# Macaron block on one Trainium2 core: two halves of a split in one slot tile, a last unit in pieces of two batches, and instruction lists anew

## The reference, cut to what matters

```python
x = L0_attn_hidden_states                       # (8, 256, 128)
x = x + 0.5 * ffn(layernorm(x))
x = x + attn(layernorm(x))
x = x + 0.5 * ffn(layernorm(x))                 # same weights again

def ffn(x):                                     # 8 experts, top 2, capacity 40 per batch
    probs = softmax(x @ Wr); topk_probs, topk_experts = top_k(probs, 2)
    pos = position of the token among those of its expert (cumulative count); keep = pos < 40
    buf[e, b, pos] += x                         # dispatch
    h = relu(einsum('ebnc,ech->ebnh', buf, W1) + b1)
    y = einsum('ebnh,ehc->ebnc', h, W2) + b2
    return sum over k of y[e, b, pos] * keep * topk_probs

def attn(x):                                    # 16 heads, feature dim 16, head dim 8
    q, k, v = x @ Wq / 4, x @ Wk, x @ Wv
    # quadratic attention, causal: weights (q.k)**2, normalised by their sum + 1e-5
    return o @ Wo
```

## Time and profile before

| | |
|---|---|
| median of 3 runs | 193.42 us (193.16 to 193.84) |
| profiled execution | 193.27 us, span 191.5 us, granted TensorE clock 1.0 |
| PE busy | 179.5 us (94%), 2253 matmuls |
| ACT busy | 150.4 us (79%) |
| DVE busy | 135.6 us (71%) |
| POOL busy | 66.5 us (35%) |

### The profile page before, as it was taken

One profiled execution on the slowest core, in us unless ns is written; L12 is line 12 of the kernel. 1 busy time (PEld: TensorE's weight loads), 2 busy tenths in 40 slices (PEclk: granted clock), 3 DMA queues, 4 the chain that ended last, 5 costly groups with the idle time before them and its releaser, 6 DMA issues.

```text
span 191.5 us, 5890 instructions
## 1 busy us (share of the span) xinstructions
PE 179.5 (94%) x2253; PEld 139.4 (73%) x2253; DVE 135.6 (71%) x400; ACT 150.4 (79%) x357; POOL 66.5 (35%) x102
## 2 busy tenths in 40 slices
PE   7976999999999999999999899999999999999962
PEld 7954899799979855555555555555599998999952
DVE  0999858968888588559466676879488887365162
ACT  3788999768768698998998889898799675993830
POOL 8904762800000036654854558679300000000000
PEclk9999999999999999999999999999999999999999
DMA  4999900530016896379476825614400008003003
GB/s 139 330 326 316 230 15 0 99 69 3 0 35 187 221 239 204 106 201 240 133 207 194 236 80 157 184 45 82 82 3 0 3 0 168 0 5 109 0 5 110
DMA packets 34284, 22.82 MB, mean 119 GB/s; under 512 B 14248, under 2 KB 31184, under 8 KB 34256
## 3 DMA queue, kind: packets, MB, share of 16 engines
q1 hardware_dynamic: 34112, 22.44, 44.5%
q10 hardware_dynamic: 144, 0.00, 0.0%
HBM read 14.05 MB, written 5.24 MB: 101 GB/s over the span
## 4 chain that ended last, share of the span: by engine, by line
PE 84%; DVE 8%; ACT 4%; issue 1%; POOL 1%; DVEq 0%; ACTq 0%; POOLq 0%
PE psB L1007 18%; PE psB L1077 9%; PE psS L1060 6%; PE psS L888 5%; PE psB L898 5%; PE psS L890 4%; PE psS L889 4%; PE psB L983 4%; PE psB L1079 4%; PE psB L1098 3%; PE psB L1016 3%; PE psB L950 2%; PE psB L888 2%; PE psB L1088 2%; PE psB L890 2%; PE psB L889 2%
## 5 line engine op out<-in xcount | busy, mean ns | idle before, releaser
L554 POOL TENSOR_SCALAR_AFFINE_SELECT amat<-amat 128x512 f32<-128x512 f32 x64 | 44.1, 697 | 55.4 <-ACT amat L637 54.5
L637 ACT ACTIVATE amat<-psS 128x768 f32<-128x768 f32 x64 | 50.1, 820 | 5.8 <-PE psS L1062 5.3
L608 ACT ACTIVATE hid<-psS,biasT 128x160 f32<-128x160 f32 x128 | 39.9, 404 | 9.6 <-PE psB L1007 4.8
L1007 PE MATMUL psB<-hid,w 128*128 128x160 f32 x256 | 40.4, 305 | 0.3 <-issue 0.2
L1007 PEld LDWEIGHTS psB<-hid,w 128*128 128x128 f32 x256 | 35.5, 190 | 1.4 <-issue 1.1
L888 PE MATMUL psS<-xe,w 128*128 128x160 f16 x128 | 27.1, 232 | 1.6 <-DVE xe L343 1.3
L889 PE MATMUL psS<-xe,w 128*128 128x160 f16 x128 | 27.1, 233 | 0.0
L890 PE MATMUL psS<-xe,w 128*128 128x160 f16 x128 | 27.1, 233 | 0.0
L1077 PE MATMUL psB<-amat,vst 128*32 128x256 f32 x256 | 20.4, 390 | 0.0
L1060 PE MATMUL psS<-stack 64*128 64x256 f16 x128 | 17.3, 278 | 0.9 <-ACT amat L637 0.8
L616 ACT ACTIVATE yT<-psB,biasT 128x160 f32<-128x160 f32 x32 | 12.6, 413 | 6.6 <-PE psB L1007 6.5
(11 more groups left out here) (151 smaller groups left out, 349.9 us busy)
## 6 DMA issues: line engine op xcount, KB each, us to landing
qk_parts<-qk SPq DMA_DIRECT2D x16, 256.0 KB, 3.5
stack<-qk_parts SPq DMA_DIRECT2D x16, 256.0 KB, 3.7
stack<-qk_parts SPq DMA_DIRECT2D x32, 128.0 KB, 3.8
amat<-in_L_ffn_W SPq DMA_DIRECT2D x8, 256.0 KB, 4.9
w<-in_L_ffn_W SPq DMA_DIRECT2D x8, 256.0 KB, 5.1
x<-in_L_attn_hidden_states SPq DMA_DIRECT2D x4, 256.0 KB, 4.6
out<-x SPq DMA_DIRECT2D x8, 128.0 KB, 1.8
amat<-in_L_attn_Wq SPq DMA_DIRECT2D x1, 128.0 KB, 4.8
```

What stands on the lines that cost most here:

```text
L554: pool.affine_select(out=d, in_=d, pattern=[[0, 2], [0, 2], [1, P]], compare_op=ALU.is_ge, fill=0.0, base=0, channel_multiplier=-1).then_i ...
L608: ins = act.activation(hid[:, n % 2, c, :], psS[:, wide_slot(s) + c // 2, (c % 2) * GS:(c % 2 + 1) * GS], ACT.Relu, bias=biasT[:, e * HC + ...
L637: act.activation(amat[:, n % A_RING, :, :], psS[:, wide_slot(s):wide_slot(s) + 2, 0:T + P], ACT.Square)\
L1007: ins = mm(bank(s)[:, 0:GS], w2[:, e, c, :], hid[:, n % 2, c, :], start=(c == 0), stop=(c == HC - 1))
```

## The change

Four things.

The third slot tile: rows 0 to 63 of `y16[:, 0]` hold the high half of slots 256 to 319, rows 64 to 127 the low half of the same slots, and combine does one matmul where it did two. For that `yT` has the columns of the last 64 slots twice (ACT writes the results of experts 6 and 7 to two places, through a broadcast source), `ohT` has its rows 0 to 63 again in rows 64 to 127 (a DMA for each half of a unit, stage `od` on SP, semaphore `doubled`, for which combine waits), and the slot weights are made for both halves: pw's matmuls of the third tile are written as two, for output partitions 0 to 63 and 64 to 127, and the mask `pmask` gets the second half in the setup on POOL.

The last unit: from slot tile 1 on, y is handled in pieces of two batches (`yt.1.1.1` to `yt.1.1.4`). The weight is applied by ACT while it rounds, per batch, straight from PSUM, and again by DVE while it subtracts. `ca` falls in three: tile 0, then tile 1 for either pair of batches.

The stores of batches `1.1.1` and `1.1.3` leave from ACT's queue.

The four tables are new lists.

```diff
+        def slot_parts(k):
+            n = P if k < KT - 1 else P // 2
+            return [(slice(r, r + n), slice(k * P, k * P + n)) for r in range(0, P, n)]
...
+                elif s[0] == "od":
+                    _, l, g, h = s
+                    u = units.index((l, g))
+                    sp.wait_ge(turned[h], 16 * (u + 1))
+                    if u:
+                        sp.wait_ge(doubled[h], 16 * u)
+                    rows = slice(h * GT // 2, (h + 1) * GT // 2)
+                    sp.dma_start(ohT[P // 2:P, parity(l, g), rows, KT - 1, :],
+                                 ohT[0:P // 2, parity(l, g), rows, KT - 1, :]).then_inc(doubled[h], 16)
...
+                    if e == E - 1:
+                        act.wait_ge(y_taken, n)
+                    if (e + 1) * CAP > (KT - 1) * P:
+                        dst = yT[:, parity(l, g), :, e * CAP:e * CAP + P].rearrange("p b (a c) -> p b a c", a=2)[:, :, :, 0:CAP]
+                        src = src.unsqueeze(2).broadcast_to([P, GB, 2, CAP])
...
+                    if scaled(s):
+                        act.wait_ge(slots_ready, len(units))
+                        wait_ready(act, s)
+                        rows = weighted(s)[1]
+                        for i in range(rows.start, rows.stop):
+                            full, p, hi = by_batch(s, i)[0:3]
+                            ins = act.activation(hi, full, ACT.Copy, scale=p)
...
+                elif kind == "cb":
+                    store(act, s)
...
+                        for i in range(rows.start, rows.stop):
+                            full, p, hi, lo = by_batch(s, i)[3:]
+                            ins = dve.scalar_tensor_tensor(out=lo, in0=full, scalar=p, in1=hi, op0=ALU.mult, op1=ALU.subtract)
...
-                        for a in range(2):
+                        for a in range(1 if k == KT - 1 else 2):
...
-                                last = mm(m[:, o:o + 2 * E], oh[:, parity(*s[1:]), TT * i + t, k * P:(k + 1) * P],
-                                          p16[:, TT * i + t, :, :], start=(t == 0), stop=(t == TT - 1))
+                                for rows, cols in slot_parts(k):
+                                    last = mm(m[rows, o:o + 2 * E], oh[:, parity(*s[1:]), TT * i + t, cols],
+                                              p16[:, TT * i + t, :, :], start=(t == 0), stop=(t == TT - 1))
...
-yt.1.1.1 yt.1.1.2 yt.1.1.3 ca.1.1 cb.1.1.0 cb.1.1.1 cb.1.1.2 cb.1.1.3
+ca.1.1.0 yt.1.1.1 yt.1.1.2 yt.1.1.3 yt.1.1.4 ca.1.1.1 ca.1.1.2 cb.1.1.0 cb.1.1.1 cb.1.1.2 cb.1.1.3
```

More of the change, by code:

```diff
@@ L85 @@
[L85 to L89, removed]
@@ L310, in macaron_program @@
         turned = [sem(f"turned{c}") for c in range(2)]
+        doubled = [sem(f"doubled{c}") for c in range(2)]
+        slots_ready = sem("slots_ready")
         stored = sem("stored")
@@ L377, in weighted, with scaled, low_rows @@
             _, l, g, k = stage
-            if (l, g) == units[-1] and k >= KT - 1:
-                half = k - (KT - 1)
-                return KT - 1, slice(half * GB // 2, (half + 1) * GB // 2)
+            if (l, g) == units[-1] and k:
+                half = (k - 1) % 2
+                return (k + 1) // 2, slice(half * GB // 2, (half + 1) * GB // 2)
             return k, slice(0, GB)
+        def scaled(stage):
+            return stage[1:3] == units[-1] and stage[3] > 0
+        def low_rows(k):
+            return (slice(P // 2, P), 0) if k == KT - 1 else (slice(0, P), 1)
         def weighted_in(stage):
@@ L386, in weighted_in, with by_batch @@
             w = (rows.stop - rows.start) * P
-            return (yp[:, nth[stage] % 2, 0:w].rearrange("p (b c) -> p b c", c=C),
-                    y16[:, 0, rows, k * P:(k + 1) * P], y16[:, 1, rows, k * P:(k + 1) * P])
+            low, a = low_rows(k)
+            full = yp[:, nth[stage] % 2, 0:w].rearrange("p (b c) -> p b c", c=C)
+            return full, y16[:, 0, rows, k * P:(k + 1) * P], full[low], y16[low, 0, rows, k * P:(k + 1) * P], y16[low, a, rows, k * P:(k + 1) * P]
+        def by_batch(stage, i):
+            _, l, g, _ = stage
+            k, rows = weighted(stage)
+            j = i - rows.start
+            low, a = low_rows(k)
+            full, p = bank(("yt",) + stage[1:])[:, j * P:(j + 1) * P], pslot[:, parity(l, g), i * KT + k:i * KT + k + 1]
+            return full, p, y16[:, 0, i, k * P:(k + 1) * P], full[low], p[low], y16[low, 0, i, k * P:(k + 1) * P], y16[low, a, i, k * P:(k + 1) * P]
         def bank(stage):
@@ L422, in in_half, with store @@
             return 4 * (pair // 4) + 2 * (pair % 2) + (pair % 4) // 2
+        def store(eng, s):
+            _, _, g, i = s
+            wait_taken(eng, s)
+            b = g * GB + i
+            eng.dma_start(out[b].rearrange("(t p) c -> p t c", p=P), x[:, TT * b:TT * b + TT, :]).then_inc(stored, 16)
         block = ctx.enter_context(nc.Block())
```

197 lines of the change are left out of this document (108 added, 89 removed).

## The result

The changed kernel takes 190.72 us (median of 4 runs, 190.53 to 191.24). The kernel before, run beside it, takes 193.63 (193.16 to 193.94). The ratio is 0.9856, with a 95% interval of 0.9824 to 0.9887: 2.9 us or 1.4% less. The forecast was 192.7 in a range of 190.3 to 194.7, with "faster" as the likeliest of the three outcomes. The time lies in the range and on the side that was given most, but 2.0 us under the forecast, near the end that was given to rival A. The profiled execution took 191.24 us, against 193.27 before.

The account below looks back on a forecast made before the run. TensorE was taken to bound the kernel, except in the tail. Terms -1.3 + 4.0 - 1.9 - 0.3 + 0.2 - 1.2 = -0.5 us took 193.42 to 192.9, leaned to 192.7; range 190.3 to 194.7.

Parts of the forecast that it names:

- rival A: Slot weights: switching to narrow parts costs nothing or half; four stages cost 0.8 us, not 4.0; 189.7 or 191.3; chance 0.22.
- Combine, -1.3: Combine outside the last unit: 10 matmuls a batch instead of 12, 24 x 0.056 us saved on TensorE.
- Slot weights, +4.0: Four slot-weight stages: eight form changes at 0.10 us plus eight more matmuls, +1.0 us each (+0.8 to +5.5 in all).
- rival E: Slot weights: each form change costs the whole length of the matmul before; 5.5 us in all, 194.2; chance 0.10.
- The lists in attention, -1.9: Attention: paired scores and values make 21 fewer form changes at 0.10 us; from 0 to -2.3 us.
- at the start, -0.3: First experts: two TensorE gaps go (-0.8 us), but expert 3's down-projection waits for ScalarE; -0.8 to +0.5 us.
- Double copy of y: Results of experts 6 and 7 written twice: +0.13 us a copy, +0.2 us in all (0 to +0.8).
- Doubling ohT, 0: Four small DMAs a layer on SP's queue land before combine needs them: 0 us, at worst +1.
- The tail, -1.2: After the last down-projection: pieces on ScalarE and VectorE, tile 0 in idle time, last store issued at 188.0, not 189.17 us.
- rival D: Combine waits for the DMA that doubles ohT: +1 us, 193.7; chance 0.05.
- Rival C: Tail: ScalarE's pieces run one after the other and nothing is gained; 194.1 us at worst, 193.7 half way; chance 0.08.
- Rival B: Attention is held by ScalarE, squares first, so the saved form changes give nothing; 194.8 us; chance 0.15.

Follow-up runs that it names:

- e4: The kernel before with only the slot weights' third tile written in two parts of 64 columns: 196.34 us, ratio 1.0162 to the kernel before.
- e5: The changed kernel with the slot-weight matmuls grouped by form, all of 128 columns first, then all of 64: 188.19 us, ratio 0.9734 to the kernel before.
- e10: The changed kernel with five score and value pairs in attention taken apart into turns on TensorE: 191.98 us, ratio 0.9949 to the kernel before.
- e3: The changed kernel with the attention and unit lists of before: 195.67 us, ratio 1.0124 to the kernel before.
- e7: The changed kernel with all four last stores on SP's queue instead of two on ACT's: 190.54 us, ratio 0.9861 to the kernel before.
- e6: The changed kernel with combine of slot tile 0 behind the last transposes instead of ahead: 189.40 us, ratio 0.9815 to the kernel before.

## Why the prediction was right, and where its sizes were off

The forecast time was 2.0 us too high. The two large misses, slot weights and lists, were both too pessimistic and the tail, 0.4 too optimistic, took little of it back; the range was wide enough to hold them. So the outcome rests on a path and on terms that were right, and on sizes of which the largest was not. Of the signs that were named, the slot weights (1.40 us, nearest to the 1.6 that was given), the fewer "issue" waits, the pieces and the DMA came out; attention shortened by 3.2 us and not by 1.5 to 2.

- **The path.** TensorE's row sets the time up to T: right. The stages' sum explains -2.03 of the profile and the tail the other -0.8.
- **Combine, -1.3.** Measured -1.25. Right.
- **Slot weights, +4.0.** The mechanism (changes of form, e4 and e5) was right, the size too large: 1.40 us a stage instead of 1.6, +3.15 in all. The price of a change, taken as 0.10, is 0.095 (e5). What was too dear was the other part: the eight matmuls more were put at 0.2 us a stage, but the two narrow ones of a pair start 0.003 us apart, so 16 full and 16 narrow ones without changes are 0.83 - 0.19 = 0.64 us, 0.04 more than the 24 full ones. Then 0.60 + 0.04 + 8 x 0.095 = 1.40. (The expectation of e5 has 0.075 a change, since it takes the narrow matmuls at 0.025; it gave 188.7 where 188.19 was measured.) Rival A (0.8 a stage) and rival E (2.0) are out.
- **The lists in attention, -1.9, and at the start, -0.3.** This is the step that failed by most. In the stages' sums the lists gave -3.9 and not -2.2. The count of 21 changes was right and its price somewhat low: by e10's 0.12 to 0.13 they are 2.5 to 2.8 us. The prediction counted the changes and held the waits in between to be unchanged. They were not. Five score stages that took 0.54 to 0.68 us take 0.18 to 0.27 now, and of the 32 down-projections seven had lasted 1.23 us or more and one does now. At the start the gain did not come: the first down lasts 1.13 and not 1.59 us, as foretold, but the transposes of the router's input and the slot weights wait instead. Up to the first score the changed kernel is 1.55 us longer, with +1.6 for two slot-weight stages and -0.4 for combine, so the lists there are +0.4 and not -0.3. The rows that show it, among TensorE's waits of the changed kernel from 18 to 71 us:

```profile
PE psB L1028 <- DVE xTf L799: 0.9, 1, 0.9
PE psB L1045 <- issue: 0.6, 1, 0.6
```

- **Terms that don't add.** The prediction put a price on each part and summed. The lists alone are worth -2.9, the rest alone +2.3 (e3), and both -2.9. What it had to say, as far as the profiles show, was that the new lists put the slot weights of unit (0, 1) between q and k and the first score, where TensorE meets the stack's DMAs, so that their cost falls into a wait. It looked for no wait at that place.
- **Double copy of y.** The wide copies make the line's mean 0.440 us where it was 0.413, eight of 32 being wide: (32 x 0.440 - 24 x 0.413) / 8 = 0.52 each, +0.11 where +0.13 was taken.
- **Doubling ohT, 0.** Right: combine waits for no DMA, and rival D is out. The eight land 2.3 us after issue:

```profile
ohT<-ohT SPq DMA_DIRECT2D x8, 64.0 KB, 2.3
```

- **The tail, -1.2.** Measured -0.8. Each step came as written: ScalarE's start at T + 1.8 (forecast T + 1.8), its pieces (2.19 - 0.40) / 7 = 0.26 apart (0.27; the 0.40 is the forecast's length of one), VectorE's end at T + 4.8 (T + 4.7), the last store at T + 6.3 (T + 6.2). Rival C is out. What failed is the last step, a landing as long as before: the store landed 2.20 us behind its issue and not 1.94, which takes back 0.3 of the 0.4 that "could" be, and e7 shows the second queue to bring 0.2 us at most for that reason. And it took the place of tile 0's combine for free, which costs 1.0 us (e6).
- **Rival B**, attention held by ScalarE: out. ScalarE is busy 95% of attention, and yet the waits for its squares went down.
- **Slips in the sums.** The rivals are counted from two bases: A, B and C from 192.9, D and E from 192.7. C's 194.1 puts the tail's gain at nothing, where the prediction's own worst case of +0.4 would give 194.5. Neither moves a verdict.

What stays open: why the changed kernel's waits for ScalarE are shorter with a busier ScalarE. The pairs in TensorE's list and ScalarE's own new order came together. e10 took five of the pairs apart and the waits stayed at 2.5 us, so it isn't those; the order of ScalarE and VectorE was not tried by itself. Of the microsecond that is lost or found at the first score, the part of a late landing and that of TensorE's coming early were not told apart by repeated profiles.

## What to carry to other kernels

Count the changes of matmul form along TensorE's order, price them from the trace (0.09 to 0.13 us each here), and order or group the matmuls by form before looking for anything cleverer: grouping one loop was worth 2.3 us of 190. Where an edit fills time and another makes the engine arrive earlier somewhere, look at the next DMA that it will meet there, and don't add the two prices; the same lists were worth 2.9 us or 5.2. In a tail, whatever stands ahead of the instruction that starts the last chain is on the path, even if the engine had been idle a moment later.

## What the runs showed of the hardware

A change between the forms of 128 by 128 and 128 by 64 costs 0.095 us, the mean of both ways (e5), one in attention 0.12 to 0.13 (e10). The two narrow matmuls of a pair, which write output partitions 0 to 63 and 64 to 127, start 0.003 us apart, and pairs follow each other every 0.032 us (e5), where full ones of 16 moving columns are 0.025 apart: the pair works nearly side by side, and gains nothing on the full form. For four last stores of 128 KB each, two queues gave an issue 0.46 us earlier and a landing 0.26 us longer than one (e7). And the time at which TensorE reaches its full clock differs from execution to execution, by 3 us in eleven of the twelve profiles (3.95 to 7.10 us) and by 10 in one (14.04), which moves everything behind it by 1.0 and by 3.9 us.
